# A graph-attention and routed-expert kernel: turned x copied two pairs later in the last two heads, q computed earlier, sums copied by bank, small operations of the experts spread

## The chip, the cores and the metric
The kernel runs on one core of a Trainium2 chip. The metric is the device time of one execution in microseconds, lower being better.

## What is computed
x is 1024 tokens of width 512. Four layers follow each other, each taking the layer norm of x and adding its result to x:
```
x = x + _L0_gnn_ref(_layernorm(x), edge_index, ...)
x = x + _L0_ffn_ref(_layernorm(x)[None], ...)[0]      # 64 experts, top 2
x = x + _L1_gnn_ref(_layernorm(x), edge_index, ...)   # two graph attentions
x = x + _L1_ffn_ref(_layernorm(x)[None], ...)[0]      # 8 experts, top 1
```
The change lies in the third and the fourth. A graph attention with 8 heads is
```
h = (x @ W).reshape(N, heads, out_ch)
e = leaky_relu(a_src[src] + a_dst[dst], 0.2)
ex = exp(e - m[dst])                      # m: the largest e of each dst
out = segment_sum(h[src] * ex / s[dst])   # s: the sum of ex of each dst
```
once with out_ch 128 (a relu behind it) and once with 64 (a log-softmax over the 512 columns behind it). The experts of the last layer send each token to the expert with the largest router logit, `relu(xf @ W1[e] + b1[e]) @ W2[e] + b2[e]`, weighted by its gate.

## The kernel before
The program gives each of the five engines its own list of instructions, ordered by hand, with semaphores between them. No scheduler sorts anything: tables of pairs in the Python code (`TURN`, `SUM`, `ev`, `Q_AFTER`, `H_AFTER`) say behind which pair an extra piece of work is issued.

Both attentions are written by one function, `attend`. The edges are held as a dense 1024 x 1024 matrix CT that is added ahead of the exponential (absent edges very negative). The work is 64 *pairs*, pair (hd, s) being head hd and the source tile s of 128 tokens, with number k = 8*hd + s. For a pair:
- GpSimd adds the target's row qb to CT (`am<-CT,qb`, L2306). Its ring has four buffers, so it waits for the exponential of pair k-4; at a head's first pair it waits for the DMA that brings qb.
- ScalarE computes the relu of scores into PSUM (L2328), one pair ahead, then the exponential into PT (L2335).
- VectorE adds PSUM and am (`counted`, L2433) and finds maxima for a head further on (L2426, L2427, with `mrow`). In some pairs it also divides the sums of the head before (`normed`, L2442 to L2458).
- TensorE multiplies PT with h: in the second attention by `columns` (L2539), two halves of 512 columns into PSUM banks 0 and 1, summed over the head's eight pairs; in the first by `gather` (L2526). It also makes the h of later heads (`h_tile`, L2511), and rows of scores (L2499, L2504).

In the second attention, when a head is complete, ScalarE's `moved` (L2342) copies the 65 x 1024 sums from banks 0 and 1 to a_oT, and TensorE turns them by `rows` (L2550). The next head's first columns write the same banks, so they wait for the copy. For q (L2268 to L2273) GpSimd does five small operations on the maxima of a head; SP writes q to q_scratch (L2241) and reads it back as the row qb (L2244), after the row of scores `adb` (L2237) of that head in its queue.

The class `Tail` weaves the last layer into heads 6 and 7 of the second attention. There TensorE turns the residual x by four 128 x 128 transpositions into PSUM bank 6 (`turn_x`, L1775); VectorE copies the 512 columns to xcT (`x_moved`, L1919); TensorE multiplies them with the router's weights (`sum_x`, L1780). There are six such steps, two halves for each of three blocks of columns. VectorE also takes x (`taken`, L1901), adds biases with a running maximum (`biased`, L1907 and L1908) and collects statistics (L1912). After the attention come the router and then 15 blocks of 128 tokens, one for each of 8 experts and 7 more for experts with many tokens. For block e GpSimd fetches rows (L1708), VectorE normalizes them (`normed(e)`, L2019), TensorE turns them (L1845), VectorE copies that (`turned(e)`, L2026), TensorE makes the hidden part (L1878), ScalarE its relu (L1763), TensorE the output (L1857), VectorE adds b2 (`moved`, L2035) and gates (`gated`, L2041), ScalarE finishes (`finished`, L1752), and GpSimd scatters (`store`, L1714). Between the first of these VectorE works out, in small operations (L2057 to L2091), where each token stands in a block.

## Time and profile before
| what | us |
|---|---|
| median of 3 runs | 1260.65 (1257.49 to 1263.9) |
| the profiled execution | 1262.32 |
| its span | 1260.6 |
| first attention, pairs | 694 to 880 |
| second attention, pairs | 924 to 1163 |
| of these, heads 6 and 7 | 1076.77 to 1163.00 |
| router, and filling of the experts | 1163 to 1196 |
| experts | 1196 to 1250 |
| last store issued | 1255.38 |

Over the span TensorE is busy 84%, VectorE 61%, GpSimd 50%, ScalarE 42%; the mean clock granted to TensorE is 0.899 of full speed. Times are read from one profiled execution on its one core, counted from the start of its span; they stand in microseconds. "Idle before" at a row is the time in which that engine did nothing ahead of it, with what ended it. "x4" is the number of instructions in a row.

### The profile page before, as it was taken

Reading aid. Unit: us, or ns where it says so; the run is one execution under the profiler, and the core shown is the slowest. Engines: PE = TensorE matmul, PEld = TensorE weight load, DVE = VectorE, ACT = ScalarE, POOL = GpSimd, SP = SyncE. Lnnn points to the kernel's source line nnn. Section 1 sums busy time; section 2 is a strip of 40 time slices with the busy share of each in tenths; the row PEclk is TensorE's granted clock in tenths of the full one; section 3 lists DMA queues with packets and bytes.
Section 4 is the critical chain, followed back from the end, with each engine's and each line's share of the span. In section 5 each row is a group of like instructions: output and inputs, shape, how many; then the busy total and the mean of one; then the engine's idle time right before and its main releaser. Section 6 shows DMA issues by size and latency. Waiting matters only on the chain. (4 is left out here: it accounts for less than half of the span.)

```text
span 1260.6 us, 17829 instructions
## 1 busy us (share of the span) xinstructions
PE 1059.0 (84%) x5581; PEld 752.3 (60%) x5581; DVE 770.9 (61%) x1724; ACT 523.9 (42%) x744; POOL 624.6 (50%) x503
## 2 busy tenths in 40 slices
PE   3999899878799999995797888888888888546696
PEld 1454677767577777773454788787654444222574
DVE  6898487537233333332976799974577777725754
ACT  2243553321111111111233688887366776525323
POOL 1000549105476555544203788996587786623233
PEclk9999899755799999997798799999799899968698
DMA  3000003056489999963201112210111111621541
GB/s 113 1 0 1 1 1 134 1 185 217 145 292 301 300 304 306 300 207 122 94 1 36 32 37 67 69 35 17 45 57 45 34 51 34 185 100 45 166 142 50
DMA packets 107987, 134.57 MB, mean 107 GB/s; under 512 B 30240, under 2 KB 76040, under 8 KB 107792
## 3 DMA queue, kind: packets, MB, share of 16 engines
q1 hardware_dynamic: 92720, 112.68, 27.7%
q0 software_dynamic: 15200, 21.04, 5.1%
q8 instruction: 36, 0.59, 0.2%
...
## 5 line engine op out<-in xcount | busy, mean ns | idle before, releaser
L2306 POOL TENSOR_TENSOR am<-CT,qb 128x1024 f32<-128x1024 f32 x128 | 301.7, 2370 | 100.8 <-ACT PT L2335 79.6
L2328 ACT ACTIVATE PS<-adb,ab 128x1024 f32<-128x1024 f32 x128 | 143.1, 1118 | 126.1 <-DVE am L2433 125.0
L2539 PE MATMUL PS<-PT,h 128*65 128x512 f32 x256 | 134.9, 667 | 57.6 <-ACT PT L2335 38.7
L2433 DVE TENSOR_TENSOR am<-PS,am 128x1024 f32<-128x1024 f32 x128 | 156.5, 1222 | 39.9 <-ACT PS L2328 27.8
L2427 DVE CUSTOM_DVE_ANT_0 masked<-PS,mask 128x1024 f32<-128x1024 f32 x128 | 156.2, 1220 | 35.7 <-issue 34.0
L2526 PE MATMUL PS<-h,PT 128*128 128x129 f32 x1024 | 131.2, 287 | 22.6 <-DVE o L2458 11.4
L1232 DVE COPY yo<-PS 128x512 f32<-128x512 f32 x64 | 44.3, 692 | 168.5 <-PE PS L1170 163.1
L2335 ACT ACTIVATE PT<-am,as 128x1024 f32<-128x1024 f32 x128 | 145.1, 1134 | 0.3 <-DVE am L2433 0.3
L2526 PEld LDWEIGHTS PS<-h,PT 128*128 128x128 f32 x1024 | 124.6, 200 | 30.4 <-issue 19.4
L1197 ACT ACTIVATE hT<-PS,b1T 128x128 f32<-128x128 f32 x128 | 40.0, 363 | 215.2 <-PE PS L1162 199.9
L1162 PE MATMUL PS<-xgT,w1r 128*128 128x128 f32 x1024 | 126.1, 277 | 0.0
L1162 PEld LDWEIGHTS PS<-xgT,w1r 128*128 128x128 f32 x1024 | 120.7, 193 | 0.8 <-issue 0.8
L1170 PE MATMUL PS<-w2r,hT 128*128 128x512 f32 x256 | 120.3, 593 | 0.0
L2539 PEld LDWEIGHTS PS<-PT,h 128*65 128x65 f32 x256 | 35.7, 152 | 133.9 <-issue 108.1
L1098 POOL DMA_INDIRECT ys_scratch<-yo,r_rowsi x64 | 65.2, 1019 | 99.7 <-DVE yo L1232 89.1
L485 DVE TENSOR_SCALAR oh_src<-iota,eT 128x1024 f16 x150 | 72.6, 484 | 13.3 <-PE PS L697 8.2
...
L697 PE MATMUL PS<-oh_src,oh_dst 128*128 x300 | 66.6, 379 | 0.4 <-issue 0.4
L1170 PEld LDWEIGHTS PS<-w2r,hT 128*128 128x128 f32 x256 | 43.8, 191 | 31.1 <-issue 31.1
L2511 PEld LDWEIGHTS PS<-W2t,x2T 128*128 128x128 f32 x384 | 55.1, 194 | 11.1 <-issue 7.6
L2511 PE MATMUL PS<-W2t,x2T 128*128 128x128 f32 (+1 forms) x384 | 60.1, 315 | 0.0
L1223 DVE COPY xgT<-PS 128x512 f32<-128x512 f32 x64 | 43.6, 681 | 19.7 <-PE PS L1153 19.5
...
## 6 DMA issues: line engine op xcount, KB each, us to landing
...
```

The source lines that it names most:

```text
L485: dve.tensor_scalar(oh_src[:, bass.ds(slot, 1), c, :], iota[:], eT[:, 0, c, bass.ds(q, 1)], None, ALU.is_equal)
L697: mm = pe.matmul(PS[:, 2 * (t % 2) + h, :], oh_dst[:, bass.ds(slot, 1), c, :], oh_src[:, bass.ds(slot, 1), c, h * 512:(h + 1) * 512], star ...
L1162: mm = pe.matmul(PS[:, 2 + j % 2, c * P:(c + 1) * P], w1r[:, j, k, c * P:(c + 1) * P], xgT[:, j % 2, k, :], start=(k == 0), stop=(k == KD ...
L1170: mm = pe.matmul(PS[:, 4 + j % 2, :], hT[:, j % 2, c, :], w2r[:, j, c, :], start=(c == 0), stop=(c == HC - 1))
L2306: pool.tensor_tensor(am[:, k % RING, :], CT[:, s, :], qb[:, hd % 2, :], ALU.add).then_inc(s_sum, 1)
L2328: act.activation(RELU, adb[:, hd % 2, :], ACT.Relu, bias=ab[:, s, hd:hd + 1]).then_inc(s_relu, 1)
L2335: act.activation(PT[:, k % PR, :], am[:, k % RING, :], ACT.Exp, bias=as02[:, s, hd:hd + 1], scale=1 - NEG_SLOPE).then_inc(s_exp, 1)
L2427: dve.tensor_tensor_reduce(masked[:], wide(row_bank(hd)), mask[:, t, :], 1.0, -3.0e38, ALU.subtract, ALU.max, mrow[:, hd % 2, t:t + 1]).th ...
L2433: dve.tensor_tensor(am[:, k % RING, :], RELU, am[:, k % RING, :], ALU.add).then_inc(s_all, 1)
L2511: mm = pe.matmul(PS[:, bank, columns_out], xT[:, k, tile * P:(tile + 1) * P], W[half][:, k, columns_in], start=(k == 0), stop=(k == KI - 1))
L2526: mm = pe.matmul(PS[:, d // PER, (d % PER) * (CH + 1):(d % PER + 1) * (CH + 1)], PT[:, (NT * hd + s) % PR, d * P:(d + 1) * P], h[:, s, hd, :],
L2539: mm = pe.matmul(PS[0:CH + 1, half, :], h[:, s, hd, :], PT[:, (NT * hd + s) % PR, half * 512:(half + 1) * 512], start=(s == 0), stop=(s == ...
```

## The change
- **Turned x** (`TURN`, `SUM`, the new `MOVE`). Transpositions were issued behind pairs (6,2), (6,4), (6,5), (6,6), (6,7), (7,0), and VectorE copied five of six in the pair of the same name; now transpositions stand behind every second pair, (6,2) to (7,4), the sums one pair later, and the copies two pairs later than the transpositions.
- **q** (`Q_AFTER`). GpSimd computes q of heads 2 to 7 behind the first pair of the head before instead of behind its third, in both attentions.
- **Sums by bank** (`moved`, `columns`). ScalarE copies banks 0 and 1 apart, the first as soon as TensorE has done its half of the last pair (`s_half`); the next head's halves wait each for their own copy.
- **First attention's start.** The last h copied ahead of the loop (`h_moved(H0 - 1)`) stands behind the first relu instead of behind the first exponential.
- **Experts.** VectorE's order at the start: five small operations ahead of normed(0), normed three blocks ahead instead of two, the other small operations as `places()` behind block 0's step and `owners()` in block 2's. Gating and finishing lag by one block instead of three from block 6 on (`gated_at`). For the last block, b2 times the gate plus x and the shift (`sc[2]`) are added to xg ahead of time by VectorE and ScalarE, and one VectorE operation from PSUM gives the output.

```diff
@@ -1559,8 +1559,10 @@
...
-            TURN = {(6, 2): (0, 0), (6, 4): (0, 1), (6, 5): (1, 0), (6, 6): (1, 1), (6, 7): (2, 0), (7, 0): (2, 1)}
-            SUM = {(6, 4): (0, 0), (6, 5): (0, 1), (6, 6): (1, 0), (6, 7): (1, 1), (7, 0): (2, 0), (7, 1): (2, 1)}
+            TURN = {(6, 2): (0, 0), (6, 4): (0, 1), (6, 6): (1, 0), (7, 0): (1, 1), (7, 2): (2, 0), (7, 4): (2, 1)}
+            SUM = {(6, 3): (0, 0), (6, 5): (0, 1), (6, 7): (1, 0), (7, 1): (1, 1), (7, 3): (2, 0), (7, 5): (2, 1)}
+            MOVE = {(6, 4): (0, 0), (6, 6): (0, 1), (7, 0): (1, 0), (7, 2): (1, 1), (7, 4): (2, 0), (7, 6): (2, 1)}
...
+            def gated_at(self, e):
+                return {0: (), 1: (), 2: (), 3: (0,), 4: (1, 2), 5: (3, 4)}.get(e, (e - 1,))
...
                 def store(e):
-                    pool.wait_ge(self.s_fin, e + 1)
+                    if e < NB1 - 1:
+                        pool.wait_ge(self.s_fin, e + 1)
+                    else:
+                        pool.wait_ge(self.s_last, 1)
...
                     a.then_inc(self.s_hhm, 1)
-                    if e >= 3:
-                        finished(e - 3)
-                for e in range(NB1 - 3, NB1):
-                    finished(e)
+                    if e == NB1 - 1:
+                        act.wait_ge(self.s_rest, 1)
+                        g = self.xg8[:, e % self.G8, :]
+                        act.activation(g, g, ACT.Identity, bias=self.sc[:, 2, e:e + 1]).then_inc(self.s_restm, 1)
+                    for i in self.gated_at(e):
+                        finished(i)
@@ -1933,9 +1945,8 @@
...
-                ev = {(6, 3): (0, 0), (6, 4): (0, 1), (6, 5): (1, 0), (6, 6): (1, 1), (6, 7): (2, 0), (7, 0): (2, 1)}
-                if (hd, s) in ev:
-                    self.x_moved(dve, *ev[hd, s])
+                if (hd, s) in self.MOVE:
+                    self.x_moved(dve, *self.MOVE[hd, s])
                 if hd == 6 and s >= 4:
                     for t in (2 * (s - 4), 2 * (s - 4) + 1):
                         self.biased(dve, t, 0, A)
@@ -2051,45 +2062,52 @@
...
-                normed(0)
-                normed(1)
-                turned(0)
                 link(dve.tensor_copy(self.rki[:], self.rk[:]))
                 dve.tensor_scalar(self.hii[:], self.rki[:], P.bit_length() - 1, None, ALU.logical_shift_right)
                 link(dve.tensor_scalar(self.loi[:], self.rki[:], P - 1, None, ALU.bitwise_and))
                 dve.tensor_copy(self.hif[:], self.hii[:])
                 link(dve.tensor_copy(self.lof[:], self.loi[:]))
-                link(dve.tensor_tensor(self.wx[:], self.M[:], all_rows(self.beg), ALU.mult))
-                link(dve.tensor_reduce(self.begt[:], self.wx[:], X, ALU.add))
-                turned(1)
+                normed(0)
+                normed(1)
+                turned(0)
                 normed(2)
                 for t in range(NT):
                     i = dve.tensor_scalar(self.R2[:, t, :], self.iota128[:], self.lof[:, t:t + 1], None, ALU.is_equal)
                 link(i)
-                link(dve.tensor_scalar(self.col[:], self.hif[:], 0.0, -64.0, ALU.is_equal, ALU.mult))
-                link(dve.tensor_tensor(self.begt[:], self.begt[:], self.hif[:], ALU.add))
-                link(dve.scalar_tensor_tensor(self.col[:], self.begt[:], -1.0, self.col[:], ALU.add, ALU.add))
...
-                link(dve.tensor_tensor(self.jc[:], self.jx[:], self.cum[:].unsqueeze(1).to_broadcast([P, MORE, NX1]),
-                                       ALU.is_ge))
-                link(dve.tensor_reduce(self.own[:], self.jc[:], X, ALU.add))
-                link(dve.tensor_scalar(self.own[:], self.own[:], float(NX1 - 1), None, ALU.min))
-                dve.tensor_copy(self.owni[:], self.own[:]).then_inc(self.s_own, 1)
...
-                i.then_inc(self.s_rhs2, 1)
+                turned(1)
+                normed(3)
+                def places():
+                    link(dve.tensor_tensor(self.wx[:], self.M[:], all_rows(self.beg), ALU.mult))
+                    link(dve.tensor_reduce(self.begt[:], self.wx[:], X, ALU.add))
...
+                    dve.wait_ge(self.s_gate, 1)
...
+                    i.then_inc(self.s_rhs2, 1)
+                def owners():
+                    link(dve.tensor_tensor(self.jc[:], self.jx[:], self.cum[:].unsqueeze(1).to_broadcast([P, MORE, NX1]),
...
+                    dve.tensor_copy(self.owni[:], self.own[:]).then_inc(self.s_own, 1)
...
@@ -2098,10 +2116,14 @@
                     ofs[e] = self.expert(dve, e)
                     if e and e + 1 < NB1:
                         turned(e + 1)
-                    if e and e + 2 < NB1:
-                        normed(e + 2)
+                    if e and e + 3 < NB1:
+                        normed(e + 3)
                     if e:
                         moved(e - 1, ofs[e - 1])
+                    if e == 0:
+                        places()
+                    if e == 2:
+                        owners()
...
-                    if e >= 3:
-                        gated(e - 3)
-                gated(NB1 - 3)
-                gated(NB1 - 2)
-                moved(NB1 - 1, ofs[NB1 - 1])
-                gated(NB1 - 1)
+                    for i in self.gated_at(e):
+                        gated(i)
+                    if e == NB1 - 2:
+                        n = NB1 - 1
+                        g = self.xg8[:, n % self.G8, :]
+                        dve.wait_ge(self.s_xn, NB1)
+                        dve.scalar_tensor_tensor(g, self.b2b[:, self.expert(dve, n), :].rearrange("p o d -> p (o d)"),
+                                                 self.sc[:, 3, n:n + 1], g, ALU.mult, ALU.add).then_inc(self.s_rest, 1)
+                n = NB1 - 1
+                dve.wait_ge(self.s_y, NB1)
+                dve.wait_ge(self.s_restm, 1)
+                dve.wait_ge(self.s_st[n % 4], 16 * (n // 4))
+                dve.scalar_tensor_tensor(self.yo4[:, n % 4, :], PS[:, 4 + n % 2, :], self.sc[:, 3, n:n + 1],
+                                         self.xg8[:, n % self.G8, :], ALU.mult, ALU.add).then_inc(self.s_last, 1)
...
             A_ROW = {0: 2, **{8 * (hd - 3) + 6: hd for hd in range(3, HEADS)}}
-            Q_AFTER = {1: 1, **{NT * (hd - 1) + 2: hd for hd in range(2, HEADS)}}
+            Q_AFTER = {1: 1, **{NT * (hd - 1): hd for hd in range(2, HEADS)}}
...
-                        act.wait_ge(s_O, NT * hd + NT)
                         wait(act, s_tr, hd)
-                        act.copy(oT[:], PS[0:CH + 1, 0:2, :].rearrange("p a n -> p (a n)")).then_inc(s_oT, 1)
+                        for half in range(2):
+                            act.wait_ge(s_half if half == 0 else s_O, hd + 1 if half == 0 else NT * hd + NT)
+                            act.copy(oT[:, half * 512:(half + 1) * 512], PS[0:CH + 1, half, :]).then_inc(s_oT, 1)
...
@@ -2384,14 +2416,14 @@
                     act.wait_ge(s_bm, 2)
                     act.wait_ge(s_q0m, 1)
                     relu(0)
-                    for i in range(max(2, H0 - 3), H0 - 1):
+                    for i in range(max(2, H0 - 3), H0 - 1 if final else H0):
                         h_moved(i, unit_bank(i))
                     for k in range(PAIRS):
                         hd, s = k // NT, k % NT
                         if k + 1 < PAIRS:
                             relu(k + 1)
                         exp(k)
-                        if k == 0:
+                        if final and k == 0:
                             h_moved(H0 - 1, unit_bank(H0 - 1))
...
                     def columns(hd, s):
-                        if s == 0:
-                            wait(pe, s_oT, hd)
                         h_ready(hd, s)
                         pe.wait_ge(s_exp, NT * hd + s + 1)
                         for half in range(2):
+                            if s == 0:
+                                wait(pe, s_oT, 2 * hd - 1 + half)
                             mm = pe.matmul(PS[0:CH + 1, half, :], h[:, s, hd, :],
                                            PT[:, (NT * hd + s) % PR, half * 512:(half + 1) * 512], start=(s == 0),
                                            stop=(s == NT - 1))
+                            if half == 0 and s == NT - 1:
+                                mm.then_inc(s_half, 1)
                         mm.then_inc(s_O, 1)
                     def rows(hd, moved):
-                        pe.wait_ge(s_oT, hd + 1)
+                        pe.wait_ge(s_oT, 2 * hd + 2)
```

On TensorE, in heads 6 and 7 of the second attention, before (a_oT holds a head's sums, xcT the turned x, wrc the router's weights):
```order
L2550 MATMUL PS<-ident,a_oT 128x65 x8
L1775 MATMUL PS<-ident,x_res 128x128 x4
L2539 MATMUL PS<-PT,h_8228 65x512 x4
L1780 MATMUL PS<-wrc,xcT 128x8 x4
L1775 MATMUL PS<-ident,x_res 128x128 x4
L2539 MATMUL PS<-PT,h_8228 65x512 x2
L1780 MATMUL PS<-wrc,xcT 128x8 x4
L1775 MATMUL PS<-ident,x_res 128x128 x4
L2539 MATMUL PS<-PT,h_8228 65x512 x2
```

and now, from the same place:
```order
L2584 MATMUL PS<-ident,a_oT 128x65 x8
L1787 MATMUL PS<-ident,x_res 128x128 x4
L2571 MATMUL PS<-PT,h_8228 65x512 x2
L1792 MATMUL PS<-wrc,xcT 128x8 x4
L2571 MATMUL PS<-PT,h_8228 65x512 x2
L1787 MATMUL PS<-ident,x_res 128x128 x4
L2571 MATMUL PS<-PT,h_8228 65x512 x2
L1792 MATMUL PS<-wrc,xcT 128x8 x4
```

The second transposition stood right behind the sums of the first; now a pair's columns stand between the sums and it, and each pair has either the sums or the transpositions.

On VectorE, pairs (6,5) and the head of (6,6), before:
```order
L2433 TENSOR_TENSOR am<-PS,am 128x1024
L1901 TENSOR_TENSOR x_res<-x_res,a_zo 128x4x128
L1919 COPY xcT<-PS 128x512
L1907 MEMSET spare 128x1
L1908 ISA a_zo,zmax<-a_zo,a_bias 128x256
L1908 ISA zmax 128x1
L1907 MEMSET spare 128x1
L1908 ISA a_zo,zmax<-a_zo,a_bias 128x256
L1908 ISA zmax 128x1
L2433 TENSOR_TENSOR am<-PS,am 128x1024
```

and now, the same pairs:
```order
L2465 TENSOR_TENSOR am<-PS,am 128x1024
L1913 TENSOR_TENSOR x_res<-x_res,a_zo 128x4x128
L1919 MEMSET spare 128x1
L1920 ISA a_zo,zmax<-a_zo,a_bias 128x256
L1920 ISA zmax 128x1
L1919 MEMSET spare 128x1
L1920 ISA a_zo,zmax<-a_zo,a_bias 128x256
L1920 ISA zmax 128x1
L2465 TENSOR_TENSOR am<-PS,am 128x1024
L1913 TENSOR_TENSOR x_res<-x_res,a_zo 128x4x128
```

The copy to xcT has gone from between the taking of x (L1901, now L1913) and the bias operations in pair (6,5).

On GpSimd, in the attention (ab and a2p are scores' parts, q the result), before:
```order
L2306 TENSOR_TENSOR am<-CT,qb 128x1024 x5
L2268 TENSOR_TENSOR zx<-mrow,ab 128x8
L2269 TENSOR_SCALAR zy<-zx 128x8
L2270 TENSOR_TENSOR zx<-zx,zy 128x8
L2271 TENSOR_TENSOR zx<-ab,zx 128x8
L2273 TENSOR_SCALAR q_6047<-zx 128x8
L2306 TENSOR_TENSOR am<-CT,qb 128x1024 x3
L2316 TENSOR_TENSOR ab_6059<-ab_6059,a2p 128x128
```

and now:
```order
L2338 TENSOR_TENSOR am<-CT,qb 128x1024 x3
L2300 TENSOR_TENSOR zx<-mrow,ab 128x8
L2301 TENSOR_SCALAR zy<-zx 128x8
L2302 TENSOR_TENSOR zx<-zx,zy 128x8
L2303 TENSOR_TENSOR zx<-ab,zx 128x8
L2305 TENSOR_SCALAR q_6047<-zx 128x8
L2338 TENSOR_TENSOR am<-CT,qb 128x1024 x5
L2348 TENSOR_TENSOR ab_6059<-ab_6059,a2p 128x128
```

The five small operations of q have moved two `am` ahead.

## Rows read from the trace of the kernel before
**Rows 1.** Stretches: us, busy us (count) of each engine, granted clock, DMA share, GB/s.
```profile
1076.77:1163.00 86.23, 50.79 (x168) 21.69 (x166) 43.90 (x109) 36.87 (x35) 37.42 (x24) 0.80 0.32 106
1196.00:1250.00 54.00, 54.00 (x327) 39.89 (x325) 29.76 (x53) 15.91 (x37) 19.30 (x18) 1.00 0.34 110
```
**Rows 2.** Waits, 1076 to 1163 (engine line <- what ended them: us, times, longest).
```profile
DVE xcT L1919 <- PE PS L1775: 34.0, 5, 8.1
```
**Rows 3.** Timeline of one pair of head 6 (start, us, what, idle before).
```profile
1119.86 1.22 DVE L2433 TENSOR_TENSOR am<-PS,am 128x1024 f32<-128x1024 f32 x1
...
1121.18 1.12 ACT L2328 ACTIVATE PS<-adb,ab 128x1024 f32<-128x1024 f32 x1 [7.93 <-DVE am L2433]
...
1123.51 3.65 PE L2539 MATMUL PS<-PT,h 128*65 128x512 f32 x4 [5.00 <-ACT PT L2335]
...
1128.72 0.69 DVE L1919 COPY xcT<-PS 128x512 f32<-128x512 f32 x1 [7.64 <-PE PS L1775]
...
1130.04 1.22 DVE L2433 TENSOR_TENSOR am<-PS,am 128x1024 f32<-128x1024 f32 x1
```
**Rows 4.** Timeline of VectorE, pairs of heads 6 and 7.
```profile
1087.23 2.77 DVE L1901 TENSOR_TENSOR x_res<-x_res,a_zo 128x512 f32<-128x512 f32 x1
...
1090.52 1.21 DVE L2433 TENSOR_TENSOR am<-PS,am 128x1024 f32<-128x1024 f32 x1
...
1099.91 1.21 DVE L2433 TENSOR_TENSOR am<-PS,am 128x1024 f32<-128x1024 f32 x1
1101.05 0.68 DVE L1901 TENSOR_TENSOR x_res<-x_res,a_zo 128x512 f32<-128x512 f32 x1
...
1143.30 1.22 DVE L2433 TENSOR_TENSOR am<-PS,am 128x1024 f32<-128x1024 f32 x1 [0.37 <-ACT PS L2328]
...
1145.78 1.22 DVE L2433 TENSOR_TENSOR am<-PS,am 128x1024 f32<-128x1024 f32 x1 [0.47 <-ACT PS L2328]
```
**Rows 5.** Timeline at a head boundary, a clock window, a later wait.
```profile
1003.64 1.01 ACT L2342 COPY a_oT<-PS 65x1024 f32<-65x1024 f32 x1
...
1004.70 6.60 PE L2539 MATMUL PS<-PT,h 128*65 128x512 f32 x11 [2.42 <-ACT a_oT L2342]
...
1004.67:1008.08 3.41, 3.38 (x4) 0.98 (x5) 2.54 (x6) 3.12 (x3) 2.52 (x2) 0.50 0.00 0
...
1075.34 1.90 PE L2539 MATMUL PS<-PT,h 128*65 128x512 f32 x4 [1.66 <-ACT PT L2335]
```
**Rows 6.** Timeline at the start of the first attention.
```profile
695.34 1.12 ACT L2328 ACTIVATE PS<-adb,ab 128x1024 f32<-128x1024 f32 x1 [5.42 <-DVE am L2433]
...
697.44 0.56 ACT L2359 COPY h<-PS 128x512 f32<-128x512 f32 x1
...
698.05 1.03 PE L2499 MATMUL PS<-a,sel 80*128 80x512 bf16 x2 [7.01 <-ACT h L2359]
```
**Rows 7.** Timeline of GpSimd and VectorE, last head of the first attention.
```profile
853.86 9.31 POOL L2306 TENSOR_TENSOR am<-CT,qb 128x1024 f32<-128x1024 f32 x4 [2.34 <-DMA qb<-q_scratch]
...
856.24 1.22 DVE L2433 TENSOR_TENSOR am<-PS,am 128x1024 f32<-128x1024 f32 x1 [3.25 <-POOL am L2306]
```
**Rows 8.** Timeline of GpSimd and VectorE, head 2 of the second attention.
```profile
992.88 2.36 POOL L2306 TENSOR_TENSOR am<-CT,qb 128x1024 f32<-128x1024 f32 x1 [3.77 <-ACT PT L2335]
...
994.06 1.22 DVE L2427 CUSTOM_DVE_ANT_0 masked<-PS,mask 128x1024 f32<-128x1024 f32 x1
...
1002.52 1.22 DVE L2433 TENSOR_TENSOR am<-PS,am 128x1024 f32<-128x1024 f32 x1
```
**Rows 9.** Timeline of the experts' start and end.
```profile
1195.64 0.55 PE L1845 MATMUL PS<-ident,xn 128*128 128x128 f32 x3 [1.15 <-DVE xn L2019]
...
1246.58 3.60 PE L1857 MATMUL PS<-w2x,hTx 128*128 x8
...
1251.52 0.98 POOL L1714 DMA_INDIRECT out<-yo,x_picked  x1 [2.52 <-ACT yo L1752]
...
1255.38 0.98 POOL L1714 DMA_INDIRECT out<-yo,x_picked  x1 [0.30 <-issue]
```

37 lines of the change are left out of this document (23 added, 14 removed).

## The prediction
> **What bounds the kernel now.** I started with the table of stretches. In the routed experts after 1196 TensorE is busy in all of the 54.00 us at clock 1.00. In heads 6 and 7 of the second attention (1076.77 to 1163.00) no engine is full: TensorE 50.79 of 86.23 us, VectorE 43.90, at a granted clock of 0.80 [rows 1]. So this stretch is bound by a chain, and the table of waits names it: VectorE's copy of the turned x waits five times for TensorE's transposition (L1775), 34.0 us in all, 8.1 at most [rows 2].
>
> The timeline shows the ring: VectorE's `counted` at 1119.86, ScalarE's activation at 1121.18 after 7.93 us of idling, then the exponential, TensorE's column products at 1123.51, behind them the router's sums and the four transpositions, and at 1128.72 VectorE's copy, which had waited 7.64 us. After the copy and two bias operations, 1.3 us in all, the next `counted` starts at 1130.04: one pair takes 10.18 us [rows 3]. Nothing overlaps, since the copy in a pair wants the transposition that TensorE does behind that same pair's columns. Without it a pair takes 2.48 us (1143.30 to 1145.78) [rows 4]. `counted` of pair (6,4) starts at 1090.52 and that of (7,2) at 1143.30, six pairs in 52.8 us [rows 4].
>
> **The change, part by part.**
> *Transpositions and copies in heads 6 and 7.* The same six transpositions, six sums and six copies; each copy now stands two pairs behind its transposition. Is the distance enough? From ScalarE's activation to the columns are 2.3 us, and columns, sums and transpositions are done 5.2 us after that (1123.51 to 1128.72), with the columns' products at half clock (3.65 us for four) [rows 3]. The whole road is 1.3 + 2.3 + 5.2 = 8.9 us from the start of `counted`. The copy two pairs later comes after two pairs (2 x 2.48 or more), its own `counted` (1.1) and often 0.6 of another operation: 6.7 or more. A sum no longer follows the columns of the same pair as its transposition, and at full clock the four take 1.90 as at 1075.34 [rows 5], so that with the sums (some 1.2 of the 5.2) gone too the road is near 5.9. I take the wait as gone at full clock and expect up to 2 us where the clock is low.
>
> What the pairs cost then is VectorE's own work, by distances between starts: `counted` 1.14 (1099.91 to 1101.05), taking 0.65, a copy of turned x with two 256-wide bias operations 1.3, so 0.6 and 0.7 [rows 3, 4]; the normalization of head 5 in (6,4) I put at 1.0, its largest operation being as wide as the copy. Pair (6,4): 1.14 + 1.0 + 0.6 + 0.7 = 3.5; (6,5) 2.5; (6,6) 1.14 + 0.65 + 0.6 + 0.7 = 3.1; (6,7) 2.5 (the cadence); (7,0) 2.7; (7,1) 2.5; together 16.8. Three copies now fall into (7,2), (7,4) and (7,6), and one leaves (6,3): +0.1 net, since in such a pair VectorE idles (0.37 us before 1143.30, 0.47 before 1145.78 [rows 4]).
>
> On top comes a cost that the lockstep hides. VectorE's taking of x took 2.77 us at 1087.23, while GpSimd ran `am`, and 0.68 at 1101.05, when GpSimd stood: 2.1 for one collision [rows 4]. In the dense order GpSimd works nearly always, so there may be one such stall in each of the six pairs: between 0 and 6 x 2.1 = 12.5 us. I take the middle, 6.3: the row at 1101.05 was with GpSimd standing, so the trace bounds the share of pairs that meet it from neither side. The six pairs then take 16.8 + 6.3 = 23.1, and the change saves 52.8 - 23.1 - 0.1 = **29.6** (range 23 to 36).
> The Trainium skill, "SBUF — State Buffer", section "SBUF: two separate sides", says why: a VectorE operation with two SBUF inputs and a GpSimd operation that reads SBUF hold the shared ports by an exclusive lock for the whole instruction, whichever starts first. By that rule this change, which packs both engines' work, would meet a stall in nearly each pair, not in half of them, and the saving would be the low end of the range; the trace agrees in kind (2.77 against 0.68), and does not show how often.
>
> *Sums copied by bank.* In heads 1 to 5 of the second attention TensorE waits for the 65x1024 copy: 2.42 us at 1004.70, the copy being 1.01 (1003.64) [rows 5]. A 512-wide copy is 0.56 (697.44) [rows 6], so the first half of the columns may start some 0.45 sooner, and the second copy runs beside it. ScalarE pays 2 x 0.56 - 1.01 = 0.1 more, which is small beside its idling. I count 5 x 0.44 = 2.2, and 0.4 at the last head, where only the rows wait: **2.6** (0 to 3.5, zero if the wait merely moves to the exponential that TensorE needs as well).
> *The clock behind it.* After the wait of 2.42 us the granted clock is 0.50 (1.2 GHz) from 1004.67 to 1008.08; the first four 512-wide products after a wait of 1.66 (1075.34) take 1.90 us, against 3.65 for four in the ring, so there it stayed at full clock (2.4 GHz) [rows 3, 5]. Five head boundaries have such a low stretch of 3.41 us, and it costs half its length, 1.7. The shortened waits of about 2.0 lie between the idle time that left the clock up and the one that did not. I take two of five as kept: **3.4** (0 to 8.5).
>
> *q two pairs sooner.* GpSimd's five small operations come two `am` earlier, so the scores' row reaches q_scratch and returns sooner. In the first attention GpSimd waited 2.34 us for qb at 853.86, and VectorE then 3.25 for GpSimd at 856.24, of which 1.26 is the usual wait for ScalarE, so near 1.8 is lost [rows 7]; one other head loses some 0.4. Gain **2.2** (1 to 3.8). GpSimd pays with a possible wait for the head's last maximum: in head 2 of the second attention that is at 994.06, 1.2 long, the five operations after it take 1.4, so the next `am` (992.88 now) would start at about 996.8, 3.9 later, and end at 999.2. The `counted` that reads it is at 1002.52 [rows 8]: 3.3 us in hand, no cost.
>
> *Start of the first attention.* ScalarE's copy of the last h piece now stands before the first exponential. TensorE waited 7.01 us for that copy, which ran at 697.44, while ScalarE had been idle for 5.42 us before 695.34 [rows 6]. In that gap the copy fits, and TensorE's two score products (1.03) are done before the exponential ends near 697.5; its pair products then begin some 1.3 sooner (697.6 instead of 698.9), and with the wait off its queue at most 3.7 sooner where it is the late one. I take between these ends **2.4** (1 to 3.7).
>
> *Experts.* normed(3) now stands ahead of VectorE's small operations for the places, and the four for the owners two experts later, so that turned(2) comes sooner too; TensorE waited 1.15 us for normed(3) at 1195.64 [rows 9] and needs no such wait now: **1.4** with a little from the piece before it (0.5 to 2). At the end TensorE's last products run 1246.58 to 1250.18, and four stores are issued at 1.29 us spacing from 1251.52 to 1255.38, since gating lagged three experts [rows 9]. With gating one expert behind, two stores are left; the last operation (0.75 at most, from PSUM) ends near 1251.0 and its store is issued at 1252.1, **3.3** sooner (2 to 4). The two operations added for the last expert lie under TensorE.
>
> Sum: 29.6 + 2.6 + 3.4 + 2.2 + 2.4 + 1.4 + 3.3 = 44.9. The profiled execution took 1262.32 (span 1260.6), which gives 1217.4. The median of the three runs is 1.7 below that execution; I put the forecast at **1216**.
>
> **The rivals.**
> 1. *Collisions in every pair.* VectorE's operations with two SBUF inputs meet `am` in all six pairs, and the head boundaries keep their low clock. For it: GpSimd would be busy 2.3 of every 2.5 us. Against: the bias operations are short. 1216 + 6.3 + 3.4 = 1226.
> 2. *No collisions, and the clock stays up.* The stalls fall into idle slots and none of the five boundaries drops: 1216 - 6.3 - 5.1 = 1205.
> 3. *The copy still waits.* If TensorE stays at the low clock in heads 6 and 7 (0.80 on average now [rows 1]), the road of 8.9 us is longer than the 6.7 at hand, the pairs stretch, and TensorE idles as now; 4 us in five pairs: 1216 + 20 = 1236.
> 4. *Slower.* The early q makes GpSimd wait for the last maximum at each of 12 heads. It decides from the point at which the next `am` is more than 3.3 us late [rows 8]; then VectorE, ScalarE and TensorE stop behind it. If all of the 3.9 were laid open each time, that is 12 x 3.9 = 47 us, more than the whole gain; and since TensorE then stands longer than the 2.42 us behind which its clock fell [rows 5], the six heads of the first attention would get a low stretch each, 6 x 1.7 = 10: 1216 + 47 + 10 = 1273. Against it stand the 3.3 in hand.
> 5. *Nothing gained.* Other waits (a load, qb) take the place of those removed in both attentions, and only the experts gain: 1216 + 29.6 + 2.6 + 3.4 + 2.2 + 2.4 = 1256. In the ring every engine idles for most of a pair [rows 3], which speaks against it.
>
> **How the numbers follow.** The forecast 0.62, rival 1 0.15, rival 2 0.13, rival 3 0.05, rival 4 0.03, rival 5 0.02. The range 1203 to 1232 holds the forecast, with its unknown terms, and rivals 1 and 2. A measurement of this kernel can tell about 0.5% (6.3 us) from no change. Faster by more: 0.62 + 0.15 + 0.13 + 0.05 = 0.95; within: rival 5, 0.02; slower: rival 4, 0.03.
>
> **What would show it.** VectorE's waits for L1787 (the transposition's new line) fall from 34.0 to below 5 us; `counted` from (6,4) to (7,2) spans 20 to 27 us, with some taking and bias operations of 1.5 to 2.8 us; at the head boundaries TensorE's wait is near 2.0, and the clock reads 1.00 behind some of them; GpSimd has no wait for qb over 1 us in the first attention; TensorE's wait at 698 shrinks to about 3; the last store is issued about 2 us behind TensorE's end. I am wrong if the copies still wait over 2 us each, if the pairs take 4.5 us or more, or if GpSimd waits for maxima with VectorE behind it.

## The result, and the profile after
The change makes the kernel faster: the median went from 1262.24 us (4 runs, 1257.49 to 1263.9) to 1224.11 us (4 runs, 1220.19 to 1226.61), a ratio of 0.970, 95% interval 0.966 to 0.974. The forecast was 1216, range 1203 to 1232. The profiled executions compare as 1262.32 with 1223.25, spans 1260.6 and 1221.5, so 39.1 us went. The mean granted clock rose from 0.899 to 0.916.

Where they went can be read by laying the same instruction of both traces side by side: the start of `counted` of a pair, and marks behind the attention.

| stretch | forecast | measured |
|---|---|---|
| start of the first attention, to pair (0,6) | 2.4 | 3.8 |
| rest of it, to pair (0,1) of the second (q, qb) | 2.2 | 2.6 |
| second attention to (6,2): copies by bank, clock | 5.6 | 0.9 |
| heads 6 and 7, (6,2) to (7,7) | 29.6 | 28.5 |
| to the last sums' division (last copy) | 0.4 | 0.4 |
| router, to the first block's transpositions | 0 | 0.5 |
| experts, to TensorE's end | 1.4 | -0.1 |
| TensorE's end to the last store's issue | 3.3 | 2.4 |
| sum | 44.9 | 39.0 |

The first row is counted from the start of the span, and pair (0,0) of the first attention, which the change does not touch, itself comes 1.0 us later in the changed kernel's trace (695.13 against 694.09). From pair (0,0) to pair (0,6) it is 17.5 us instead of 22.4, a gain of 4.9.

The stretches of the changed kernel that answer to [rows 1] (us, busy us and count of TensorE, weight loads, VectorE, ScalarE, GpSimd, then granted clock, DMA share, GB/s):
```profile
1069.48:1127.00 57.52, 44.48 (x168) 19.86 (x166) 50.12 (x109) 37.43 (x38) 40.00 (x20) 0.94 0.48 156
1157.00:1211.00 54.00, 52.13 (x322) 39.17 (x321) 32.44 (x58) 16.54 (x38) 19.72 (x19) 1.00 0.35 116
```
Heads 6 and 7 with their end take 57.5 us instead of 86.2, and the clock there is 0.94 instead of 0.80. In the experts TensorE is no longer without a gap: 52.13 of 54.00 us.

The table of waits of the changed kernel over heads 6 and 7, which answers to [rows 2] (engine, line, what ended the wait: us in total, times, longest):
```profile
ACT PS L2360 <- DVE am L2465: 18.9, 16, 5.8
PE PS L2571 <- ACT PT L2367: 14.0, 9, 3.8
...
POOL am L2338 <- DMA qb<-q_scratch: 3.1, 1, 3.1
PEld PS L1792 <- DVE xcT L1931: 2.9, 3, 1.7
```
No row of VectorE waiting for the transpositions (L1787 now) is left in it; 34.0 us stood there. TensorE's longest wait for ScalarE is 3.8 us, GpSimd's for qb 3.1.

VectorE's timeline over pairs (6,4) to (7,2) of the changed kernel, which answers to [rows 3, 4]:
```profile
1081.85 1.21 DVE L2465 TENSOR_TENSOR am<-PS,am 128x1024 f32<-128x1024 f32 x1
...
1084.62 2.13 DVE L1920 CUSTOM_DVE_ANT_0 a_zo<-a_zo,a_bias 128x256 f32<-128x256 f32 x1
...
1087.04 1.21 DVE L2465 TENSOR_TENSOR am<-PS,am 128x1024 f32<-128x1024 f32 x1
1088.17 0.68 DVE L1913 TENSOR_TENSOR x_res<-x_res,a_zo 128x512 f32<-128x512 f32 x1
...
1090.64 1.84 DVE L1913 TENSOR_TENSOR x_res<-x_res,a_zo 128x512 f32<-128x512 f32 x1
...
1093.02 1.96 DVE L1920 CUSTOM_DVE_ANT_0 a_zo<-a_zo,a_bias 128x256 f32<-128x256 f32 x1
...
1094.92 2.55 DVE L1920 CUSTOM_DVE_ANT_0 a_zo<-a_zo,a_bias 128x256 f32<-128x256 f32 x1
...
1101.68 1.80 DVE L1920 CUSTOM_DVE_ANT_0 a_zo<-a_zo,a_bias 128x128 f32<-128x128 f32 x1
...
1103.64 2.41 DVE L1920 CUSTOM_DVE_ANT_0 a_zo<-a_zo,a_bias 128x128 f32<-128x128 f32 x1
...
1108.67 1.23 DVE L2465 TENSOR_TENSOR am<-PS,am 128x1024 f32<-128x1024 f32 x1 [0.37 <-ACT PS L2360]
```
GpSimd's timeline in pair (6,4):
```profile
1084.11 2.36 POOL L2338 TENSOR_TENSOR am<-CT,qb 128x1024 f32<-128x1024 f32 x1
```
The six pairs last from 1081.85 to 1108.67, 26.8 us instead of 52.8. Of these, 10.2 are stalls: 2.13, 1.96 and 2.55 us for bias operations of 0.41, 1.80 and 2.41 for ones of 0.28, 1.84 for a taking of 0.68, each less what the same operation takes alone. The 16.6 that are left are near the 16.8 that the prediction gave for the pairs without stalls. The first shows what a stall is: GpSimd's `am` runs from 1084.11 to 1086.47, and the operation issued at 1084.62 ends at 1086.75. It is the same in heads 6 and 7 of all fourteen traces of this case: each of the 107 bias and taking operations that began inside an `am`, more than 0.1 us before its end, ended 0.15 to 0.56 us behind that end, and none of the others took more than 0.71. So a stall is what is left of the `am` that is running.

### The profile page after: what moved, and what is told of

The parts are those of the page before. It is cut to its first block and busy times, and to the rows that moved or that the text cites. A ratio compares the mean times of both kernels' runs of the same rounds, so it can differ in the third digit from the quotient of the medians.

```text
span 1221.5 us, 17837 instructions
## 1 busy us (share of the span) xinstructions
PE 1049.0 (86%) x5578; PEld 745.7 (61%) x5581; DVE 777.8 (64%) x1724; ACT 524.4 (43%) x752; POOL 624.5 (51%) x503
## 5 line engine op out<-in xcount | busy, mean ns | idle before, releaser
L2338 POOL TENSOR_TENSOR am<-CT,qb 128x1024 f32<-128x1024 f32 x128 | 302.0, 2382 | 29.7 <-ACT PT L2367 17.5
L2571 PE MATMUL PS<-PT,h 128*65 128x512 f32 x256 | 128.6, 636 | 34.3 <-ACT PT L2367 22.8
L2558 PE MATMUL PS<-h,PT 128*128 128x129 f32 x1024 | 127.9, 283 | 22.4 <-ACT PT L2367 12.6
L2558 PEld LDWEIGHTS PS<-h,PT 128*128 128x128 f32 x1024 | 120.9, 196 | 30.5 <-issue 18.2
L1098 POOL DMA_INDIRECT ys_scratch<-yo,r_rowsi x64 | 65.2, 1019 | 99.3 <-DVE yo L1232 88.9
L1093 POOL DMA_INDIRECT xg<-xs_scratch,r_rowsi x64 | 65.4, 1022 | 20.5 <-issue 17.5
```

What stands on the lines that cost most here:

```text
L2338: pool.tensor_tensor(am[:, k % RING, :], CT[:, s, :], qb[:, hd % 2, :], ALU.add).then_inc(s_sum, 1)
L2558: mm = pe.matmul(PS[:, d // PER, (d % PER) * (CH + 1):(d % PER + 1) * (CH + 1)], PT[:, (NT * hd + s) % PR, d * P:(d + 1) * P], h[:, s, hd, :],
L2571: mm = pe.matmul(PS[0:CH + 1, half, :], h[:, s, hd, :], PT[:, (NT * hd + s) % PR, half * 512:(half + 1) * 512], start=(s == 0), stop=(s == ...
```

## The experiments
Single executions of one kernel differ by up to 8 us, so where a part is worth less than that, the verdict is taken from the distances between the same instructions of the traces.

**The tables alone.** The kernel before with nothing but this:
```diff
-            TURN = {(6, 2): (0, 0), (6, 4): (0, 1), (6, 5): (1, 0), (6, 6): (1, 1), (6, 7): (2, 0), (7, 0): (2, 1)}
+            TURN = {(6, 2): (0, 0), (6, 4): (0, 1), (6, 6): (1, 0), (7, 0): (1, 1), (7, 2): (2, 0), (7, 4): (2, 1)}
...
-                if (hd, s) in ev:
-                    self.x_moved(dve, *ev[hd, s])
+                if (hd, s) in self.MOVE:
+                    self.x_moved(dve, *self.MOVE[hd, s])
```


> The kernel before with the tables of transpositions, sums and copies alone changed. Theory: this part carries about 28.5 us of the 38, read from the two traces as the shift between pairs (6,2) and (7,7); expected 1262.2 - 28.5 = 1233.7, and VectorE meets five or six stalls of 1.2 to 2.1 us beside GpSimd's am. Rival (the parts help each other, so that alone it brings less, since the late q holds GpSimd): 1240 or more, with GpSimd waiting 4 us or more for qb in head 7.


Measured: 1231.99 us (ratio 0.975, 0.973 to 0.977), 30.4 less than the 1262.34 beside it. From (6,2) to (7,7) 46.3 us, before 75.8, changed kernel 47.2. So this one part is the gain of heads 6 and 7, and needs none of the others. The rival is out: GpSimd waited 3.65 us for qb, and the pairs were no longer for it.

**The sums copied whole again.**
```diff
-                        for half in range(2):
-                            act.wait_ge(s_half if half == 0 else s_O, hd + 1 if half == 0 else NT * hd + NT)
-                            act.copy(oT[:, half * 512:(half + 1) * 512], PS[0:CH + 1, half, :]).then_inc(s_oT, 1)
+                        act.wait_ge(s_O, NT * hd + NT)
+                        act.copy(oT[:], PS[0:CH + 1, 0:2, :].rearrange("p a n -> p (a n)")).then_inc(s_oT, 1)
```


> The changed kernel with the 65x1024 sums copied in one piece again. Theory: TensorE's wait at a head boundary and the low clock behind it lie beside the ring of ScalarE and VectorE, so that the split copies gave 0.9 us over six heads and 0.4 at the last: 1224.1 + 1.3 = 1225.4, TensorE's waits at 2.4 us. Rival, the prediction's term: 2.6 for the copies and more where the clock was kept: 1228 or more.


Measured: 1225.71 us (0.971, 0.970 to 0.973). Here and with three other kernels the same boundary, the first columns of head 3, shows what the copy and the clock do. The changed kernel's timeline (start, us, what, idle before):
```profile
996.59 1.06 ACT L2374 COPY a_oT<-PS 65x512 f32<-65x512 f32 x2
...
997.31 7.21 PE L2571 MATMUL PS<-PT,h 128*65 128x512 f32 x12 [2.08 <-ACT a_oT L2374]
```
The low stretch behind that start (the clock is third from the end):
```profile
998.50:1001.90 3.40, 3.28 (x5) 0.76 (x4) 3.03 (x5) 3.11 (x4) 2.63 (x2) 0.51 0.00 0
```
This kernel's timeline:
```profile
997.95 7.03 PE L2570 MATMUL PS<-PT,h 128*65 128x512 f32 x12 [2.51 <-ACT a_oT L2373]
```
The stretch behind that start:
```profile
997.95:1001.30 3.35, 3.35 (x5) 0.99 (x6) 2.48 (x6) 3.06 (x4) 2.62 (x2) 0.54 0.00 0
```
The timeline of the tables alone:
```profile
1006.74 1.93 PE L2539 MATMUL PS<-PT,h 128*65 128x512 f32 x4 [2.41 <-ACT a_oT L2342]
```
Its stretch:
```profile
1006.74:1010.10 3.36, 3.11 (x7) 0.94 (x8) 2.49 (x6) 3.07 (x3) 2.46 (x2) 1.00 0.00 0
```
The timeline of the kernel with q late (below):
```profile
997.53 1.90 PE L2571 MATMUL PS<-PT,h 128*65 128x512 f32 x4 [2.08 <-ACT a_oT L2374]
```
And its stretch:
```profile
997.53:1000.90 3.37, 2.70 (x6) 0.77 (x7) 2.44 (x5) 3.08 (x4) 2.43 (x2) 1.00 0.00 0
```
The split shortens TensorE's wait from 2.4 to 2.5 us to 2.08, as forecast (0.34 instead of 0.44). But the length of that wait does not decide the clock: behind 2.41 us it stayed at 1.00 in one kernel, behind 2.51 it fell to the lower level in another; behind 2.08 it fell in the changed kernel and stayed in the one with q late. Five boundaries lie between (1,0) and (6,0). That distance is 129.4 us with whole copies and no low stretch, 129.7 with split copies and no low stretch (q late, and others), 130.7 in the changed kernel with four of them low, 131.6 in the kernel before and 132.0 here, both with whole copies and all five low. So splitting gives nothing by itself at these boundaries, and a low stretch there costs 0.2 (split) to 0.5 us (whole), not 1.7. At the last head, where only the rows wait for the copy, the split does count: from (7,7) to the last sums' division it is 6.6 us here, in the kernel before and with the tables alone, and 6.2 in the changed kernel. The theory's sizes stand: 0.4 at the last head, and 0.9 at the boundaries, where a low stretch costs less with the split and one of the five stayed high. The rival's 2.6 and more does not.

**q late again.**
```diff
-            Q_AFTER = {1: 1, **{NT * (hd - 1): hd for hd in range(2, HEADS)}}
+            Q_AFTER = {1: 1, **{NT * (hd - 1) + 2: hd for hd in range(2, HEADS)}}
```


> The changed kernel with q again behind the third pair. Theory: the first attention loses the 2.1 us again (1.8 at head 7, 0.3 at head 6) and head 7 of the second, now three times denser, waits for qb longer than the 3.1 us of the changed kernel, of which VectorE feels a part: 1226 to 1230. Rival, q is worth only what the first attention shows: 1226.


Measured: 1221.46 us (0.967, 0.966 to 0.969), no slower than the changed kernel. From (5,1) to (7,7) of the first attention it is 57.8 us, in the changed kernel 57.5, and in the kernel before 60.1; but the tables alone, with q as late as before, also had 57.8. GpSimd does wait for qb (1.63 us in the last head, against 0.26), and VectorE feels 0.3 of it. Both expectations fall: q is worth 0.3 us here, and the 2 us that the trace of before showed were that one execution's. In that trace TensorE's clock fell in this head too (0.50 from 861.3 to 864.7), and in no other trace did it fall there.

**The owners' operations early.**
```diff
                     if e == 0:
                         places()
+                        owners()
-                    if e == 2:
-                        owners()
```


> The changed kernel with the four operations for the owners right behind those for the places instead of two experts later. Theory: the seven loads of 512 KB then start some 8 us sooner and no longer pack into the 12 us in which block 8's rows are fetched (6.4 us to land); TensorE's wait of 0.64 us at 1179.48 goes: 0.9 us less, or 2.3 if the stall of 4.7 us on VectorE near 1186 comes from the same loads: 1221.8 to 1223.2. Rival: the stall has nothing to do with the loads and stays, and the four operations delay turned(2): 1224 or more.


What it was to explain stands in VectorE's timeline of the changed kernel:
```profile
1176.05 0.55 DVE L2030 TENSOR_SCALAR xn<-xg,x_sc 128x512 f32<-128x512 f32 x1 [2.88 <-DMA xg<-xs_scratch,x_picked]
...
1190.63 0.69 DVE L2046 TENSOR_TENSOR yo<-PS,b2b 128x512 f32<-128x512 f32 x1 [4.71 <-remote]
```
and in TensorE's:
```profile
1179.48 2.05 PE L1890 MATMUL PS<-xnT,w1x 128*128 128x128 f32 x16 [0.64 <-DVE xnT L2037]
...
1192.80 2.05 PE L1890 MATMUL PS<-xnT,w1x 128*128 128x128 f32 x16 [1.23 <-DVE xnT L2037]
```
Measured: 1221.58 us (0.969, 0.967 to 0.971). VectorE's wait for block 8's rows fell from 2.88 to 0.36 us, and TensorE had no wait at that place. Block 8's rows took 4.3 us from the fetch's issue to landing, against 6.5 to 6.7 in the four traces with late owners that record it. From the first transpositions to TensorE's end it took 64.1 us, instead of 65.7. Yet most of that is the other stall, of 4.71 us before 1190.63, whose releaser the profile does not know: only two of the nine traces with late owners have it, and the seven without it took 63.9 to 65.2. What does go with the late owners is the wait for block 8's rows: 2.2 to 3.5 us on VectorE in all nine, and 0.3 to 1.0 on TensorE behind it in most. So the loads in one heap cost some 0.5 us. The cause of the 4.71 stays open: that none of the five traces with early owners has it is too little to tie it to the loads, or to rule them out as the rival does.

**The last h copied late again.**
```diff
-                    for i in range(max(2, H0 - 3), H0 - 1 if final else H0):
+                    for i in range(max(2, H0 - 3), H0 - 1):
...
-                        if final and k == 0:
+                        if k == 0:
```


> The changed kernel with the last copy of h behind the first exponential again. Theory: TensorE waits 7 us for it again, pair (0,1) of the first attention starts 2.7 us later and pair (0,6) 3.8 later, and all of it is kept to the end: about 3.8 us more than the changed kernel. Rival, the prediction's middle: 2.4 more.


Measured: 1227.78 us (0.973, 0.969 to 0.976; two runs), 3.7 more than the changed kernel's median, and 5.3 more than that of its second set of runs below. From pair (0,0) of the first attention to pair (0,6) it is 22.2 us, as with the tables alone (22.2) and in the kernel before (22.4), which have the same order there; in the eleven traces with the early copy it is 17.5 to 18.1. To pair (5,1) it is 120.2, in the changed kernel 115.6 and 115.8. So the copy's place is worth 4.1 to 4.9 us: the theory's 3.8 is near but low, since it was read with the 1.0 us in it that the changed kernel's trace lost ahead of pair (0,0), and the prediction's 2.4 is out.

**Gating three blocks behind again.**
```diff
-                return {0: (), 1: (), 2: (), 3: (0,), 4: (1, 2), 5: (3, 4)}.get(e, (e - 1,))
+                return () if e < 3 else (e - 3,) if e < NB1 - 1 else (e - 3, e - 2, e - 1)
```


> The changed kernel with gating and finishing three blocks behind again (the last operation from PSUM kept). Theory: from TensorE's end to the last store's issue it takes 5.2 us instead of 2.75, so 2.4 us more; GpSimd's late stores hold nothing else. Rival: yo4's four buffers then make VectorE wait for stores, and TensorE's end is later too, 3 us or more.


Measured: 1223.41 us, the same as the changed kernel. TensorE's end to the last store takes 5.2 us instead of 2.75, as the theory says, but TensorE itself was through its blocks in 63.9 us, where the changed kernel took 65.7 (64.0 in its second trace). From the last sums' division to the last store it is 88.6 us, in the changed kernel 88.0 and 86.3. So gating early gives 2.4 at the end and may give up to 1.8 of that back on the way, when VectorE's stall falls in. The rival is out.

**The 128-wide bias operations moved away.**
```diff
-                if hd == 7 and s < 2:
-                    for t in self.half(s):
+                if hd == 7 and s == 7:
+                    for t in range(NT):
                         self.biased(dve, t, 1, B)
```


> The changed kernel with the eight 128-wide bias operations of pairs (7,0) and (7,1) moved to pair (7,7), where VectorE idles 4.2 us and GpSimd's am is over. Theory (VectorE stalls only where GpSimd reads SBUF at the same time): the two stalls in (7,0), 1.80 and 2.41 us, go and none comes in their place, the two pairs take 5.0 to 5.5 us instead of 8.7, so 3.2 to 3.7 us less in all. Rival: GpSimd or TensorE is the bound of these pairs anyway, and less than 1.5 us is gained.


Measured: 1222.39 us (two runs, 1218.33 and 1226.44; the trace is of the second). The two stalls went, and (7,0) and (7,1) take 6.5 us instead of 8.7. But from (7,2) to (7,7) it is 16.3 instead of 13.5 (14.9 in the changed kernel's second trace), so in this trace the gain is lost at once. Its timeline there:
```profile
1101.83 1.12 ACT L2360 ACTIVATE PS<-adb,ab 128x1024 f32<-128x1024 f32 x1 [5.58 <-DVE am L2465]
...
1104.16 3.65 PE L2571 MATMUL PS<-PT,h 128*65 128x512 f32 x4 [4.63 <-ACT PT L2367]
...
1113.48 0.69 DVE L1931 COPY xcT<-PS 128x512 f32<-128x512 f32 x1 [2.71 <-PE PS L1787]
```
Two stretches of it, with the clock third from the end:
```profile
1104.20:1107.60 3.40, 3.40 (x4) 1.01 (x5) 1.89 (x3) 2.66 (x3) 3.28 (x2) 0.50 0.66 248
1107.60:1111.00 3.40, 3.40 (x12) 2.15 (x11) 1.23 (x1) 2.87 (x4) 1.73 (x2) 0.50 0.00 0
```
The stalls that were left, in (6,6), held ScalarE for 5.58 us and TensorE for 4.63; behind that the clock was at 0.50, the columns took 3.65 us, and with the pairs now close VectorE waited 2.71 for the transpositions. That is the wait that the change had removed, back in one place. The theory of the stalls stands, its sum doesn't; nor is the rival right, since the two pairs did get shorter.

**One SBUF input instead of two.**
```diff
+                if heads < 7:
+                    dve.tensor_scalar(x[:, tiles, columns], x[:, tiles, columns], 1.0, None, ALU.mult).then_inc(self.s_xp, 1)
+                    return
```


> The changed kernel with x taken without its attention part in heads 6: one SBUF input (x times 1.0) in place of two (x plus the attention's output) in six operations of the same width, so the output leaves that sum out. Theory (only operations with two SBUF inputs stall): each of the six takes at most 0.7 us wherever it falls beside am; in (6,3) and (6,6) that is 1.6 and 1.2 less, though the bias operations behind them may then meet the am in their place. Rival (any operation on SBUF stalls while GpSimd runs): some of the six still take 1.5 us or more.


This kernel leaves the attention's output out of most of x, so its result is another; only the times are of use. Measured: 1222.25 us. VectorE's timeline:
```profile
1070.13 0.42 DVE L1914 TENSOR_SCALAR x_res<-x_res 128x512 f32<-128x512 f32 x1
...
1075.65 2.22 DVE L1914 TENSOR_SCALAR x_res<-x_res 128x512 f32<-128x512 f32 x1
...
1079.11 1.27 DVE L1914 TENSOR_SCALAR x_res<-x_res 128x512 f32<-128x512 f32 x1
...
1089.09 2.51 DVE L1914 TENSOR_SCALAR x_res<-x_res 128x512 f32<-128x512 f32 x1
```
GpSimd's timeline at the first two of them:
```profile
1067.84 2.36 POOL L2341 TENSOR_TENSOR am<-CT,qb 128x1024 f32<-128x1024 f32 x1
...
1075.22 2.36 POOL L2341 TENSOR_TENSOR am<-CT,qb 128x1024 f32<-128x1024 f32 x1
```
The same operation takes 0.42 us where it begins as an `am` ends (at 1070.20), and 2.22, 1.27 and 2.51 where it begins inside one; the one at 1075.65 ends at 1077.87, 0.29 us behind its `am`. So the theory falls: two inputs are not what it takes. What did not stall in any trace is the statistics (four of 128 wide, 0.86 us, one SBUF input) and the copies from PSUM (0.68). The Trainium skill, "SBUF — State Buffer", section "SBUF: two separate sides", names both kinds as taking the shared ports, an operation with two SBUF inputs and one in a two-port mode. The trace agrees with the first half; for the second no row names the mode, and that the one-input operation is the faster one (0.42 against 0.68 us for 512 columns) fits it.

**TensorE kept busy at the boundaries.**
```diff
                     def columns(hd, s):
...
+                        if s == 0 and 1 <= hd < 6:
+                            wait(pe, s_ev, hd - 1)
+                            for _ in range(10):
+                                pe.transpose(PS[:, 2, 0:P], ident[:], ident[:])
```


> The changed kernel with ten extra 128x128 transpositions of a constant (1.6 us) on TensorE ahead of the first columns of heads 1 to 5 of the second attention, in the time in which it waits 2.1 us for the copied sums. Theory: the clock then stays up behind all five boundaries, and since TensorE is not the bound of a head, that is worth 0.5 us each at most: from pair (1,0) to pair (6,0) 129.4 to 129.7 us, where four low stretches gave 130.7, and the total is within 1.5 us of the changed kernel. Rival, the prediction's price of 1.7 for each low stretch: 124 us or less for those heads, and 5 us less in all.


Measured: 1222.74 us (0.970, 0.967 to 0.972). All five boundaries stayed at the high clock, and (1,0) to (6,0) took 129.7 us. The changed kernel's second trace (next) had all five high as well, and 129.7, without the fillers. So the fillers are worth nothing that a chance doesn't give, the theory of the price stands, and the rival with its 1.7 is out. The trace's span was 1217.6 for another reason: the stalls fell in other pairs of heads 6 and 7.

**The changed kernel again.** 

> The changed kernel once more, on the chip of the two others, for comparison: 1224 (1220 to 1227). If the spread of single times comes from where the clock falls, its trace has low stretches at other places than the first time, and the distance between pairs differs there and nowhere else.


Measured: 1222.49 us (0.969, 0.967 to 0.971), and its trace had none of the four low boundaries of the first, and (7,2) to (7,7) 1.4 us longer. The expectation stands in part: the low stretches moved, and the times between pairs with them. The spread has larger parts still. From (0,1) to (1,0) of the second attention it is 20.9 us in ten traces, at clock 1.00 throughout, 22.4 in one (the last h late) with 3.4 us at clock 0.50, and 23.8 or 23.9 in three (the tables alone, the moved bias operations, and the last kernel below) with 6.8 us at 0.50. One such stretch of the moved bias operations:
```profile
921.90:925.30 3.40, 2.38 (x3) 0.76 (x4) 3.30 (x5) 3.06 (x3) 2.36 (x1) 0.50 0.05 22
```
The same four traces have one more low stretch between the two attentions, and take 51.4 or 51.5 us from (7,7) of the first to (0,1) of the second, where the ten others take 49.8. So at these places 3.4 us at the low clock cost 1.5 to 1.7 us, half their length, as the prediction priced it; only at the head boundaries do they cost less. The start of the first attention, pair (0,0), also lies anywhere from 693.5 to 697.7.

**A version from what was seen.** No bias operation beside `am`:
```diff
-                if hd == 6 and s >= 4:
-                    for t in (2 * (s - 4), 2 * (s - 4) + 1):
-                        self.biased(dve, t, 0, A)
-                if hd == 7 and s < 2:
-                    for t in self.half(s):
-                        self.biased(dve, t, 1, B)
+                if hd == 7 and s == 7:
+                    for t in range(4, NT):
+                        i = self.biased(dve, t, 0, A)
+                    self.link(dve, i)
+                    for t in range(NT):
+                        i = self.biased(dve, t, 1, B)
+                    self.link(dve, i)
...
+                for t in range(4):
+                    i = self.biased(dve, t, 0, slice(0, 2 * P))
+                link(i)
                 dve.wait_ge(self.s_T, 1)
```


> A version from what was seen: the changed kernel without any bias operation beside GpSimd's am (twelve of the sixteen in pair (7,7), where VectorE idles 4.2 us, four in its wait for the router's table), and with the owners early. Theory: the stalls of VectorE at (6,4), (6,6) and (7,0) go, TensorE no longer idles 4.6 us before (6,7) and (7,0), and its clock stays up, so the six pairs take 16 to 19 us instead of 26.8, and the end comes some 1 us later for the moved operations: 6 to 10 us less than the changed kernel. Rival (as in the run before it, where moving eight of them brought nothing): the clock falls somewhere else in these heads and VectorE waits for transpositions: within 2 us of the changed kernel.


Measured: 1209.33 us (5 runs, 1208.71 to 1213.23; ratio to the kernel before 0.959, 0.957 to 0.961), 13.2 less than the changed kernel's 1222.49 beside it. VectorE's timeline at (6,4) and (7,2):
```profile
1079.58 1.21 DVE L2468 TENSOR_TENSOR am<-PS,am 128x1024 f32<-128x1024 f32 x1
...
1095.38 1.23 DVE L2468 TENSOR_TENSOR am<-PS,am 128x1024 f32<-128x1024 f32 x1 [1.81 <-ACT PS L2363]
```
Two rows of its table of waits in heads 6 and 7:
```profile
ACT PS L2363 <- DVE am L2468: 7.6, 14, 1.3
...
PE PS L2574 <- ACT PT L2370: 4.6, 7, 1.7
```
The six pairs take 15.8 us, ScalarE waits 7.6 us in all instead of 18.9, TensorE at most 1.7 at a time, and the clock is at 1.00 in all of heads 6 and 7. From (6,2) to (7,7) it is 36.3 us (47.2). The twelve operations in (7,7) end before the last sums are there. The theory stands: 11 to 12 of the 13 us lie in these heads, more than its 6 to 10; the fallen clock went with the stalls.

**TensorE kept busy behind the attention.**
```diff
             def pe_end(self, pe):
+                fill(11)
                 pe.wait_ge(self.s_xp, 8)
...
+                fill(10)
                 pe.wait_ge(self.s_pick, 1)
...
+                fill(5)
                 pe.wait_ge(self.s_rhs, 1)
...
+                fill(32)
                 turn(0)
```


> The version before it with extra 128x128 transpositions of a constant on TensorE in its idle times behind the attention: 11 before the last transpositions of x, 10 and 5 in the waits for the router's masks, 32 in the wait of 5.4 us for the first block. Theory: the price of a low clock is nearly zero where TensorE has slack, and full where it is waited for, as here: the 16 router sums (3.58 us), the 16 products of the table (3.58), the first block's transpositions and products (1.94 and 3.79) take about half each, which is 3 to 6 us less than the version without them (1209.3). Rival: the chain here is VectorE's small operations and DMA latency, and less than 1.5 us is gained, or the fillers delay what TensorE must do.


Measured: 1211.14 us (1208.29 to 1214.44), no faster than the version. The router's sums and the table on TensorE's timeline in the version before it:
```profile
1118.88 3.58 PE L1792 MATMUL PS<-wrc,xcT 128*128 128x8 f32 x16
...
1126.06 3.58 PE L1848 MATMUL PS<-rhs,R 128*128 128x24 f32 x16 [1.16 <-DVE R L2014]
```
and here, with the first block's products:
```profile
1125.71 1.95 PE L1792 MATMUL PS<-wrc,xcT 128*128 128x8 f32 x16 [0.24 <-ACT xcT L1746]
...
1132.08 3.58 PE L1855 MATMUL PS<-rhs,R 128*128 128x24 f32 x16
...
1142.38 2.05 PE L1898 MATMUL PS<-xnT,w1x 128*128 128x128 f32 x16 [0.34 <-DVE xnT L2049]
```
The sums took 1.95 instead of 3.58 us, the first block's products 2.05 instead of 3.79 (at 1136.89 in the version's trace), but the table's still 3.58: the clock had fallen again in spite of 15 fillers. From the last sums' division to TensorE's end it is 82.3 us instead of 84.0. So 1.7 were gained, between theory (3 to 6) and rival (below 1.5). The profiled time doesn't show them: low clock in the second attention's first head, where this kernel does nothing new, took 2.9 back, and pair (0,0) of the first attention came 4.2 us later than in the version's trace.

## Why the prediction was right, and where it wasn't
*What bounds the kernel.* Right: the ring through the copy in the same pair, and its cure by two pairs of distance. VectorE's 34.0 us of waiting went to nothing, and the tables alone give 30.4 of the 38 us.

*The size of heads 6 and 7.* Near: 28.5 against 29.6, and near in part by luck, since two errors cancel. VectorE's own work (16.6 for 16.8) was right. The stalls beside GpSimd were 10.2, where the middle 6.3 stood between 0 and 12.5; rival 1, collisions in each pair, had the better number for this term. So the six pairs took 26.8 us for 23.1, or 4.47 each, just under the 4.5 that the prediction named as a sign of being wrong. The rule of the shared ports would have put a stall into nearly each pair; they came in three of six, (6,4), (6,6) and (7,0), but up to three in one. What made up for it is that (6,2) and (6,3) gained too (1.4; their taking of x stalled less, and the copy was gone) and pair (7,4) no longer waited for the last head's rows (1.2). The prediction said that the trace of before could bound the number of stalls from neither side. That trace had four of them in heads 6 and 7, though, not one (1.76 us at 1080.39, 1.54 at 1083.37, 2.77 at 1087.23, 1.70 at 1097.93), and these were all of its operations that began inside an `am`. The mechanism was read too narrowly: an operation with one SBUF input stalled as long.

*Copies by bank, and the clock behind them.* This is the step that failed: 5.6 forecast for the five boundaries (2.2 for the copies, 3.4 for the clock), 0.9 measured for both together; the 0.4 at the last head came. Two errors are in it. The low stretch of 3.41 us was priced at half its length, as though TensorE were waited for in each of them. At these boundaries it isn't: TensorE idles some 0.6 us in a pair of heads 1 to 4 when its clock is high and 0.45 to 0.5 with a low stretch in the head, so it catches up, and the price is 0.2 to 0.5. In the first head and between the attentions half the length was the right price (1.5 to 1.7). And the idle time was taken for what decides the level, "two of five"; at 2.41 and 2.51 us both outcomes were measured. The gain of the wait itself (0.34 us each) never reached the end, for the same reason.

*q two pairs sooner.* The number (2.2) came out, at 2.6, by luck: undone, it changes 0.3 us. A wait of 2.34 us for a DMA that was read once was taken for what the kernel always does. (From the rows as read, 3.25 less 1.26 is 2.0 for that head, not 1.8.) The bound on GpSimd's own wait held: VectorE never waited for it, and rival 4 did not occur.

*Start of the first attention.* 2.4 was taken, between 1 and 3.7. The table's 3.8 hides 1.0 us lost ahead of it: from pair (0,0) on it is 4.9, and 4.1 to 4.9 over the traces, so the term was too small and its range too low. TensorE's wait shrank from 7.01 to 2.61 us, as forecast, and its pair products began 1.3 us sooner after (0,0); but pair (0,1) came 3.7 us sooner, and (0,6) 4.9.

*Experts.* The first term, 1.4, is missing in the profile compared (-0.1). Of the ten traces of the new order without the unknown stall, eight show 63.8 to 64.6 us from first transpositions to TensorE's end (the two others 64.8 and 65.2), against 65.6 and 65.2 in the two with the old order: for most a gain of 0.6 to 1.8, near the forecast. What was not foreseen is that the seven weight loads, now asked for later, pack together (block 8's fetch took 6.5 to 6.7 us to land, for 4.3 to 4.5 where they don't) and that an earlier normed(e+3) waits for its rows on VectorE's queue, ahead of what TensorE needs. The end gave 2.4 instead of 3.3: the last but one store waits for ScalarE and is issued when the last operation is done too (1215.08), so the two stores end 1.3 us later than one would, as the changed kernel's timeline shows:
```profile
1210.02 3.60 PE L1869 MATMUL PS<-w2x,hTx 128*128 x8
...
1213.66 0.75 DVE L2147 SCALAR_TENSOR_TENSOR yo<-PS,x_sc,xg 128x512 f32<-128x512 f32 x1
1215.08 0.98 POOL L1724 DMA_INDIRECT out<-yo,x_picked  x1 [2.52 <-DVE yo L2147]
1216.37 0.98 POOL L1724 DMA_INDIRECT out<-yo,x_picked  x1 [0.30 <-issue]
```
These rows answer to [rows 9]: TensorE ends at 1213.62, and the last store is issued 2.75 us later, before 5.20.

*The range* held the time, 1224.11 in 1203 to 1232. The forecast was 8 us low, of which 5 are the terms of the copies and the clock.
